# An image-and-text layer on one core: the opening stage put in another order, and the sums of the output weights cut in five

## The reference

```python
# tokens: 16x16 patches -> 49 tokens of 192, plus bias and position; a class token ahead, the text behind
h = concat(cls, patches(x) @ W + b + pos, txt)              # (8, 178, 192)
# attention without a value projection, 12 heads, on layernorm(h)
Q    = xn[:, None] * W_qk[None, :, None]                    # one scale vector per head
attn = softmax(causal(Q @ Q.T / sqrt(192)))
out  = attn @ (xn - mean(wte, axis=0)) * 1/(1..178)         # wte is 50257 x 192
h    = h + concat_heads(out) @ W_o.T                        # W_o is 192 x 2304
# mixture of 16 routed experts (4 of them count per token) and a shared one, on layernorm(h)
h    = h + sum_e w_e * (silu(xt @ Wu_e) * (xt @ Wg_e)) @ Wd_e + shared
```

## Time and profile before

| | us |
|---|---|
| median of 3 runs | 526.26 (524.65 to 526.41) |
| the profiled execution, its own time | 524.14 |
| its span, first to last instruction | 522.3 |
| mean granted clock of TensorE | 0.955 |
| busy: PE, DVE, ACT, POOL | 480.4, 332.0, 178.8, 66.3 |
| share of the chain that ended last: PE, DVE, ACT | 82%, 10%, 2% |

### The profile page before, as it was taken

The page is one execution under the profiler, slowest core; times in us unless marked ns, Lnnn a source line. Parts: engine busy times, 40 slices in busy tenths (PEclk is TensorE's granted clock), DMA queues, the critical chain, the costliest instruction groups (busy, mean ns, idle before and its releaser), DMA issues.

```text
span 522.3 us, 8913 instructions
## 1 busy us (share of the span) xinstructions
PE 480.4 (92%) x2776; PEld 409.0 (78%) x2776; DVE 332.0 (64%) x868; ACT 178.8 (34%) x575; POOL 66.3 (13%) x93
## 2 busy tenths in 40 slices
PE   0689999999999999999799998779999999999995
PEld 0556666896669866697566997779999999999994
DVE  5584477716675376634863856976666666666764
ACT  0044745604556244733233013312322232223221
POOL 4011111031102011100000143000000000000000
PEclk9977899999999999999987996989999999999997
DMA  9999999489993999995000000011111111111103
GB/s 167 280 177 174 216 214 215 88 158 213 213 211 56 207 213 211 213 203 107 0 1 0 2 20 1 0 31 28 35 38 38 28 35 40 35 28 35 29 1 85
DMA packets 38618, 52.84 MB, mean 101 GB/s; under 512 B 14929, under 2 KB 31318, under 8 KB 38340
## 3 DMA queue, kind: packets, MB, share of 16 engines
q0 software_dynamic: 7664, 39.98, 37.2%
q1 hardware_dynamic: 27612, 10.64, 9.8%
q10 hardware_dynamic: 3320, 1.95, 2.0%
HBM read 50.08 MB, written 1.09 MB: 98 GB/s over the span
## 4 chain that ended last, share of the span: by engine, by line
PE 82%; DVE 10%; ACT 2%; issue 2%; ACTq 1%; DMA 1%; POOL 1%; DVEq 0%
PE bank L930 13%; PE bank L825 11%; PE bank L783 6%; PE bank L729 5%; PE bank L899 4%; PE bank L901 4%; PE bank L902 4%; PE bank L900 4%; PE bank L903 4%; PE bank L731 4%; PE bank L788 3%; PE bank L741 2%; PE bank L742 2%; PE bank L757 2%; PE bank L702 2%; PE bank L691 2%
## 5 line engine op out<-in xcount | busy, mean ns | idle before, releaser
L930 PE MATMUL bank<-wdn,hidT 128*128 128x192 f32 (+1 forms) x408 | 78.9, 330 | 5.9 <-DVE hidT L1179 5.9
L615 ACT ACTIVATE area_b<-bank,bcol 128x356 f32<-128x356 f32 x68 | 38.0, 558 | 132.3 <-PE bank L903 132.3
L1359 DVE SCALAR_TENSOR_TENSOR R<-bank,wts,R 128x192 f32<-128x192 f32 (+1 forms) x204 | 72.6, 411 | 8.2 <-issue 3.6
L930 PEld LDWEIGHTS bank<-wdn,hidT 128*128 128x128 f32 (+1 forms) x408 | 67.6, 184 | 6.5 <-DVE hidT L1179 6.5
L529 ACT ACTIVATE pm<-bank,nmax 128x128 f32<-128x128 f32 x96 | 33.9, 365 | 113.0 <-DVE nmax L1088 113.0
L825 PE MATMUL bank<-woT,oT 128*128 128x192 f32 (+1 forms) x432 | 71.6, 327 | 0.0
L1179 DVE SCALAR_TENSOR_TENSOR hidT<-bank,bcol,area_b 128x356 f32<-128x356 f32 x68 | 40.0, 588 | 48.8 <-PE bank L903 48.8
L825 PEld LDWEIGHTS bank<-woT,oT 128*128 128x128 f32 (+1 forms) x432 | 69.9, 182 | 0.5
L899 PE MATMUL bank<-xah,wah 128*128 128x356 f32 x136 | 54.3, 399 | 0.4 <-DVE lg L1137 0.4
L443 POOL DMA_DIRECT2D wacc<-in_L_attn_wte_dram x26 | 31.5, 1263 | 117.5 <-DMA wacc<-in_L_attn_wte_dram 117.5
L901 PE MATMUL bank<-xah,wal 128*128 128x356 f32 x136 | 45.2, 332 | 0.0
(11 more groups left out here) (197 smaller groups left out, 801.7 us busy)
## 6 DMA issues: line engine op xcount, KB each, us to landing
wacc<-in_L_attn_wte_dram POOLq DMA_DIRECT2D x28, 1344.0 KB, 12.9
wdn<-in_L_ffn_Wd_dram SPq DMA_DIRECT2D x16, 96.0 KB, 1.9
wacc<-wacc POOLq DMA_DIRECT2D x1, 1344.0 KB, 9.6
wra<-in_L_ffn_Wu_dram SPq DMA_DIRECT2D x16, 64.0 KB, 1.8
wrb<-in_L_ffn_Wu_dram SPq DMA_DIRECT2D x32, 32.0 KB, 2.0
wra<-in_L_ffn_Wg_dram SPq DMA_DIRECT2D x16, 64.0 KB, 2.0
wrb<-in_L_ffn_Wg_dram SPq DMA_DIRECT2D x32, 32.0 KB, 2.0
R<-in_L_attn_W_o_dram SPq DMA_DIRECT2D x2, 384.0 KB, 14.0
```

What stands on the lines that cost most here:

```text
L930: last = pe.matmul(o, hidT[:, sl, at:at + rows], wdn[:, k, :], start=True, stop=True)
L1359: last = dve.scalar_tensor_tensor(out=old, in0=src, scalar=wts[0:rows_, 3 * i + t, bass.ds(e, 1)], in1=old, op0=ALU.mult, op1=ALU.add)
```

## The change

- **Order on TensorE.** 16 products into `bank[0]` that nothing reads come first (`WARM`). `embed(0)` stands ahead of the transposes of `W_qk` and of the positions, `embed(2)` ahead of `turn_in`, and `embed(3)` ahead of `scores(0, 0)`.
- **Shifted channels.** Only pair 0 keeps the copy on VectorE, of both its images, placed at the start of VectorE's list. For images 2 to 7 all three channels are loaded a second time, 6 transfers an image in place of 4.
- **Output weights.** The lower 64 rows of chunk c and of chunk c+9 lie one above the other in a 128-partition buffer, and one transpose turns both. 18 + 18 transposes become 18 + 9. A turn now holds chunks c and c+9.
- **Stream.** GpSimd starts `wte` only after the first `rstd` and when all of `W_o` is in (`s_wo`, 12 transfers). The later `rstd` calls stand after 12, 21 chunks in place of 10, 18.
- **Zero fill** of `qb[64:P]` (64 x 4608) goes from VectorE to GpSimd. The bias transfers on ACT's queue go ahead of the positions.
- **Sum of the output weights.** One reduction over six groups becomes five additions of 128 x 576, one in each of units 0 to 4 of the last pair.

```diff
+    WARM = 16
-        wo_low = sb("wo_low", [64, NCH, P])
+        wo_low = sb("wo_low", [P, NCH // 2, P])
 def image_in(queue, b):
+            def rows_in(at, c, left):
+                dst = ximg[at:at + PS, b].rearrange("p (g w) -> p g w", g=G)
+                src = x[b, c].rearrange("(g p) w -> p g w", p=PS)
+                queue.dma_start(dst[:, :, 0:WI - left], src[:, :, left:WI]).then_inc(s_x[b // 2], 16)
             for c in range(C):
-                ...
+                rows_in((0, PS, 4 * PS)[c], c, 0)
+            for c in range(2 if b < 2 else 0, C):
+                rows_in((2 * PS, 3 * PS, 5 * PS)[c], c, HALF)
 # sync
+            heads_in(wo_high, W_o[0:P, :], NH // 2)
+            for half in range(2):
+                heads_in(wo_low[64 * half:64 * half + 64], W_o[P:E, NH * E // 2 * half:NH * E // 2 * (half + 1)], NH // 4)
 # gpsimd
+            pool.wait_ge(s_const, 1)
+            pool.memset(qb[64:P], 0.0).then_inc(s_pad, 1)
+            pool.wait_ge(s_pad, 3)
-            pool.wait_ge(s_x[0], 128)
-            pool.wait_ge(s_tokw, 64)
+            rstd(4, 1)
+            pool.wait_ge(s_wo, 16 * 12)
             pool.dma_start(wrest[0:WREST, :], wte[P * WROWS:V, :]).then_inc(wte_rest, 16)
...
 # scalar
-            for c in range(0, NCH, 2):
-                act.wait_ge(s_wops, c // 2 + 1)
-                act.activation(woT[:, c:c + 2, :], bank[4 + (c // 2) % 2][:, 0:2 * E].rearrange("p (c e) -> p c e", c=2),
+            for c in range(NCH // 2):
+                act.wait_ge(s_wops, c + 1)
+                act.activation(woT[:, c::NCH // 2, :], bank[4 + c % 2][:, 0:2 * E].rearrange("p (c e) -> p c e", c=2),
 # tensor
+            for _ in range(WARM):
+                pe.matmul(bank[0][:, :], identb[:], cmask[:].rearrange("p (a t) -> p a t", a=1).broadcast_to([P, GRP, P]),
+                          start=True, stop=True)
 def output_weights():
+                for c in range(NCH // 2):
+                    if c >= 2:
+                        pe.wait_ge(s_woT, c - 1)
+                    o = bank[4 + c % 2][:, 0:2 * E].rearrange("p (c e) -> p c e", c=2)
+                    for k in range(2):
+                        pe.transpose(o[:, k, 0:P], wo_high[:, c + NCH // 2 * k, :], ident[:])
+                    pe.transpose(o[:, :, P:E], wo_low[:, c, :], ident[:]).then_inc(s_wops, 1)
 # vector
-            dve.memset(qb[64:P], 0.0).then_inc(s_pad, 1)
+            dve.wait_ge(s_x[0], 128)
+            at = 2 * IMG - HALF
+            dve.tensor_copy(xflat[2 * PS:4 * PS, 0:at], xflat[0:2 * PS, HALF:HALF + at]).then_inc(s_shift, 1)
...
-            shift_in(0)
-            shift_in(1)
...
                     if last:
-                        if u == 1:
-                            dve.tensor_reduce(wbar[:], woT[:].rearrange("p (q c) o -> p c o q", c=3), AX.X,
-                                              ALU.add).then_inc(wbar_ready, 1)
+                        if u < 3:
+                            link(dve.tensor_tensor(wbar[:], woT[:, 0:3, :] if u == 0 else wbar[:],
+                                                   woT[:, 3 * u + 3:3 * u + 6, :], ALU.add))
+                        else:
+                            done = dve.tensor_tensor(wbar[:], wbar[:], woT[:, 3 * u + 3:3 * u + 6, :], ALU.add)
...
```

More of the change, by code:

```diff
@@ L320, in _, with heads_in @@
                 sp.dma_start(htail[TAIL * k:TAIL * k + TAIL, :, :], tails[k]).then_inc(s_text[1], 16)
-            for part, rows in ((0, P), (1, 64)):
-                src = W_o[P * part:P * part + rows, :].rearrange("o (q j e) -> o q j e", q=NH // 2, j=2)
-                dst = wo_raw[part][0:rows].rearrange("o (q c) e -> o q c e", c=3)
+            def heads_in(dst, src, q):
+                dst = dst.rearrange("o (q c) e -> o q c e", c=3)
+                src = src.rearrange("o (q j e) -> o q j e", q=q, j=2)
                 for j in range(2):
@@ L436, in _, with rstd @@
             pool.memset(wts[:], 1.0).then_inc(s_const, 1)
+            pool.wait_ge(s_const, 1)
+            pool.memset(qb[64:P], 0.0).then_inc(s_pad, 1)
+            pool.wait_ge(s_pad, 3)
+            def rstd(n, count):
+                pool.wait_ge(var_ready, count)
+                pool.tensor_tensor(rs[:, 0:n], ve[:, 0:n], mhalf[:, 0:n], ALU.pow).then_inc(rstd_ready, 1)
             def add_rows(c):
@@ L446, in add_rows @@
                     pool.dma_start(wacc[:, side], wte_v[c]).then_inc(wte_in[side], 16)
-            pool.wait_ge(s_x[0], 128)
-            pool.wait_ge(s_tokw, 64)
+            rstd(4, 1)
+            pool.wait_ge(s_wo, 16 * 12)
             pool.dma_start(wrest[0:WREST, :], wte[P * WROWS:V, :]).then_inc(wte_rest, 16)
-            def rstd(n, count):
-                pool.wait_ge(var_ready, count)
-                pool.tensor_tensor(rs[:, 0:n], ve[:, 0:n], mhalf[:, 0:n], ALU.pow).then_inc(rstd_ready, 1)
             add_rows(0)
             add_rows(1)
-            rstd(4, 1)
             rstd(4, 2)
-            for c in range(2, 10):
+            for c in range(2, 12):
                 add_rows(c)
             rstd(4, 3)
-            for c in range(10, 18):
+            for c in range(12, 21):
                 add_rows(c)
             rstd(4, 4)
-            for c in range(18, NCHUNK):
+            for c in range(21, NCHUNK):
                 add_rows(c)
@@ L695, in output_weights @@
             def output_weights():
-                pe.wait_ge(s_wo, 16 * 8)
+                pe.wait_ge(s_wo, 16 * 12)
                 pe.wait_ge(s_hin, 2)
-                for c in range(NCH):
-                    if c >= 4 and c % 2 == 0:
-                        pe.wait_ge(s_woT, c // 2 - 1)
-                    for part, rows in ((0, P), (1, 64)):
-                        last = pe.transpose(bank[4 + (c // 2) % 2][:, (c % 2) * E + part * P:(c % 2) * E + part * P + rows],
-                                            wo_raw[part][0:rows, c, :], ident[0:rows, 0:rows])
-                    if c % 2:
-                        last.then_inc(s_wops, 1)
+                for c in range(NCH // 2):
[5 more added lines that the diff above has]
+                    pe.transpose(o[:, :, P:E], wo_low[:, c, :], ident[:]).then_inc(s_wops, 1)
             pe.wait_ge(s_tokw, 64)
             embed(0)
+            pe.wait_ge(s_small, 32)
+            pe.transpose(bank[7][:, 0:NH], wqk[:, 0:P], ident[0:NH, 0:NH])
+            pe.transpose(bank[7][0:64, NH:2 * NH], wqk[:, P:E], ident[0:NH, 0:NH]).then_inc(s_wqps, 1)
+            pe.wait_ge(s_posx, 1)
+            pe.transpose(bank[4][:, 0:P], posx[:, 0, :], ident[:])
+            pe.transpose(bank[4][:, P:E], posx[0:64, 1, :], ident[0:64, 0:64]).then_inc(s_posps, 1)
             embed(1)
+            embed(2)
             def turn_in(b, bt, i):
@@ L833, in _ @@
             pe.wait_ge(s_pad, 3)
+            embed(3)
             queries_in(0, 0)
             scores(0, 0)
-            embed(2)
-            embed(3)
             output_weights()
```

37 lines of the change are left out of this document (12 added, 25 removed).

## The result

| | before | after |
|---|---|---|
| median, us (lowest to highest of 4) | 526.34 (524.65 to 527.54) | **508.35** (508.13 to 516.01) |
| ratio, with its 95% interval | | **0.966 (0.963 to 0.969)** |
| the profiled execution, its own time / its span | 524.14 / 522.3 | 508.5 / 506.7 |
| mean granted clock of TensorE | 0.955 | 0.971 |
| busy: PE, DVE, ACT, POOL | 480.4, 332.0, 178.8, 66.3 | 472.3, 322.5, 178.6, 70.5 |

The changed kernel is 3.4% faster. The fourth run after, 516.01 at a mean granted clock of 0.955, lies over 1.5% above the other three and is left out of the ratio. The profiled pair shows 15.6 us of gain, from two places. The third unit's scores start at 47.56 instead of 58.26, which is 10.7. The last pair gives 5.1. Everything between and behind those points is within 0.3 of before.

A forecast was written before the change was run, and what follows sets the result against it. It took a serial opening, paced by TensorE and ScalarE, and a VectorE reduction in the last pair as the bounds. Gains of 12.6 and 5.0 sum to 17.6: 506.5 for the profiled execution, 508.7 for the median, range 505 to 515.

The forecast's parts named there:

- The opening: From the start to the second unit's exponentials: these come at 44.1 instead of 56.70, a gain of 12.6 us.
- Embedding 0: Opening: warm-up 5.9 to 11.4, embedding ends near 14.1, VectorE picks it up at 15.84 instead of 22.00.
- Embeddings 1 and 2: Opening: images land at 16.7 and 20.2, giving some gain back; `turn_in` starts at 22.9, 4.2 ahead of 27.08.
- To the first exponentials: Opening, from `turn_in`: 8.5 instead of 10.44 without VectorE's two shifted copies, so exponentials at 31.4.
- Output weights: Opening: ScalarE's first copy at 35.0, ninth at 39.4, queries at 39.8 instead of 52.43.
- `W_o` by 30: Opening, SP's queue: the output weights land by 30, wanted at 32 to 35.
- The sum of output weights: Last pair: five additions, 3.8 in all instead of 6.09, hide in VectorE's slack; gain 5.0 us.
- That rival: Last pair: the additions aren't hidden and delay divisions and scores; the sum loses 3.8, time 512.5; chance 0.08.
- Cold and late: Opening: half-clock TensorE work and images at 18.3 leave a gain of 5.6; median 515.7; chance 0.18.
- The later date: After the opening: GpSimd's `rstd` block takes the saving back, 6 us lost, 514.7; chance 0.03.
- `W_o` late: Opening: each us of landing after 35 costs one; at 55, 528.9; chance 0.03 with any other reversal.
- signs of being wrong: Opening: image waits past 24, later embeddings at half clock, transposes 0.2 to 0.26 apart, or ScalarE's first copy awaiting `W_o`.

The follow-up runs named there:

- no warm-up: The changed kernel without the 16 opening products that nothing reads (WARM = 0): median 511.10, ratio 0.974 to the kernel before.
- mixed turns: The changed kernel with each lower chunk of output weights turned by its own transpose, 36 instead of 27: median 516.83, ratio 0.982 to the kernel before.
- lower `W_o` by ACT: The changed kernel with only the lower rows of `W_o` issued on ACT's queue behind its images: median 510.22, ratio 0.972 to the kernel before.
- the change again: The changed kernel, unaltered, measured once more on another set of runs: median 511.31, ratio 0.973 to the kernel before.
- keep warm: The changed kernel with more products that nothing reads in TensorE's waits of the opening: median 508.95, ratio 0.968 to the kernel before.
- the change a third time: The changed kernel, unaltered, measured in six more runs: median 508.69, ratio 0.969 to the kernel before.
- one sum: The changed kernel with the output weights summed in one reduction at unit 1 of the last pair: median 515.07, ratio 0.981 to the kernel before.
- only the sums: The kernel before with only the five additions in place of the one reduction: median 519.00, ratio 0.987 to the kernel before.
- third group: The last four follow-up kernels, sharing a chip; its unaltered changed kernel had median 508.69, range 507.73 to 513.23.
- keep warm, turn first: The changed kernel with filler products, `turn_in(0)` ahead of `embed(2)`, `embed(3)` behind the first scores, lower `W_o` on ACT's queue: median 507.76, ratio 0.966 to the kernel before.

## Why the prediction was right

**The opening, forecast 12.6, measured 10.7 (third scores) and 10.7 (second exponentials, 56.70 to 46.03).** The mechanism was as forecast. By its steps:

- *Embedding 0.* Warm-up from 5.96 to 11.2 (forecast 5.9 to 11.4), embedding from 11.59, picked up at 16.04 (forecast 15.84, from 22.00). Right. That the warm-up matters was not claimed as a promise; no gain of it shows in the medians (no warm-up), since the images of pair 1 land at about 17.4 with it or without.
- *Embeddings 1 and 2.* Forecast landings 16.7 and 20.2, measured 17.39 and 21.40, so `turn_in` at 24.18 for 22.9. **This is the mis-sized term: 1.3 of the 1.9.** The sum had 194 packets per us and 1.2 to land. ACT's queue was the right one to follow: SP's image of pair 1 was in by 13.4 and that of pair 2 by 16.4, while ACT's last ones, issued at 10.51 and 13.41, took 6.8 and 7.95. Its rate was faster than forecast (1353 packets by 12, 725 in the next 3 us, 768 from 15 to 18), so that by the prediction's own count packet 2152 passes at 15.3 and packet 2824 at 17.9. But the pairs landed 2.1 and 3.5 behind that. No run shows the 1.2, and the rows of before had spoken against it: by the same sum pair 1 would have been in at 15.6 there, and it was in at 17.1. What fills the lag stays open. Landings of pair 1 varied from 15.8 (mixed turns) to 17.9 (lower `W_o` by ACT).
- *To the first exponentials.* 8.44 from `turn_in`, forecast 8.5. Right. In the change again it was 11.57, at the low clock.
- *Output weights.* The first copy stands 3.54 behind the first exponentials (forecast 3.6), but from there to the queries are 5.73 for 4.8, the other 0.9. TensorE's transposes ran at half clock from 36.7 to 39.7 and let ScalarE wait 0.62 and 0.35. At full clock the term is right: in keep warm the same stretch takes 4.90 (36.66 to 41.56), and in the change a third time 4.91. Part of what is gained here is the clock's as well: in before the last nine of the 18 pairs ran at half clock, 0.70 instead of 0.46 each, 2.2 in all. "`W_o` by 30" was 5 too early; it cost little, since ScalarE came to its copy at 36.16 in any case. The pairing of lower halves is worth 4.4 at the clocks of mixed turns and of the change beside it.
- *The Trainium skill* ("TensorE: Matmul & The Clock Gate", Part 2) has weight loads pulled ahead of running products when the row groups don't conflict or the load goes to the background buffer, and the prediction weighed the reading that 128 and 64 rows can then be mixed freely. Mixed turns disagrees with that reading, though not why: a turn of two chunks takes 0.92 at full clock and 1.40 at half (two pairs of 0.46 and of 0.70), against 0.39 and 0.70 (36.70 to 37.40 after) for three transposes of 128 rows.

**The sum of output weights, forecast 5.0, measured 5.1** in the profiles of before and after; 5.3 in one sum and 5.1 in only the sums. The additions took 0.74 each and the steps between scores stay equal; behind the last unit's scores, where the additions of `wacc` stand, it is 253.2 to the end against 253.1 before. That rival is out.

**The total** was 17.6 against 15.6 between the two profiled executions. The median came to 508.35 for 508.7 because the runs of before lie 2 above their profiled one and those of after do not. Part of that hit is luck: the medians differ by 18.0, the profiled executions by 15.6, and the spread between executions made up for the 2.0 that the sum had too much.

**The rivals.** *Cold and late*, forecast 515.7 with the images of pair 1 in at 18.3, is half right: landings that late don't come, the low clock does, in some executions, and takes up to 4.2 at the third scores. One run of the first result took 516.01 and one of the third group 513.23, both at a mean clock of 0.955; neither has a profile. *The later date* doesn't bite: `rstd` ends at 104.3 and is wanted at 117.0. *`W_o` late* came true as an event (35.16) without its price. Of the prediction's signs of being wrong, TensorE waiting for images past 24 and ScalarE waiting for `W_o` don't show; transposes 0.2 to 0.26 apart do, in the four turns at half clock, and half-clock embeddings do in other executions of the same kernel. The clock also falls in the last pair and in the experts (0.53 from 262 to 269 in the first profile after), and there the same code took from 251.7 to 256.7 from its last unit's scores to the end in these profiles, so the spans of two single executions can be compared only where that part agrees, as it does in the pair of the result (253.1 and 253.2).

**What stays open.** What of TensorE's work decides in which execution the clock falls isn't settled: the Trainium skill (same page, Part 1) says that the gate's check runs freely, and the three profiles of the change (low at 36 to 40; at 18 to 22, 28 to 36 and 42 to 50; at 18 to 22 only) fit that. That it explains the spread of the medians (508.35, 511.31, 508.69) is argued, not shown, as only one run of each has a profile. Whether "keep warm, turn first" really beats the change isn't settled either. And no run puts `embed(0)` back behind `ln_w`, or the shifted copies back on VectorE: what those two edits give is read from the waits of the profiles, and not shown by taking them out.

## What to carry to other kernels

Before counting on a reordered opening, list for each step what ends its wait, down to the one transfer and when it is issued: here ACT's queue brought its image of pairs 1 and 2 in 4 and 5 us behind SP's, and TensorE waited for that one. A product moved ahead of a turn is free only if its data land in time, and a bulk stream that starts early delays the small transfers beside it. A sum that nobody needs soon should be cut into pieces that fit the slack of a unit, since a single 6 us instruction on VectorE cost 5 us of TensorE's time. Filler products kept the clock up through a sparse stretch here, but they can buy time only where TensorE's pace, and not a landing, is what ends the wait; in these medians they bought none.

## What the runs showed of the hardware

- In the changed kernel small packets fill the DMA engines (share 1.22 in this stretch) well below the byte rate that they reach later: 187 GB/s between 15 and 18, where 1315 of 1404 packets are under 512 bytes, against 407 GB/s in a stretch with the stream:

```profile
DMA packets 1404, 0.56 MB, mean 187 GB/s; under 512 B 1315, under 2 KB 1404, under 8 KB 1404
```

- In the kernel without warm-up the granted clock reads 1.00 where the first embedding takes 5.37 for 2.85:

```profile
11.00:17.00 6.00, 5.72 (x35) 3.98 (x35) 1.21 (x8) 0.12 (x1) 0.00 (x0) 1.00 1.23 201
```

  So at the start of this program the column doesn't tell the pace, and the durations do.
- One strided reduction of 128 x 3456 values into 576 takes 6.09, five additions of 576 columns 3.7 together. The zero fill of 64 x 4608 takes GpSimd 3.93 and took VectorE 3.90; it is covered on GpSimd, whose next work is at 18.77.
